# Twice x added by TensorE, the sum read from PSUM, and a tile's mean and normalisation on ScalarE

## The reference, cut to what matters

```python
xj0, xj1 = _split(node_features[col])                       # 64 scalars, 32 vectors of 3
m0, m1 = _tp(xj0, xj1, e0, e1, wm000, wm011, wm101, wm110)  # message of an edge
...
agg = segment_sum(msgs, row, num_segments=N)
u0, u1 = _tp(x0, x1, a0, a1, wu000, wu011, wu101, wu110)    # bilinear in x and agg
ud0, ud1 = _lin(x0, x1, lu0, lu1)                           # linear part
return node_features + _merge(u0 + ud0, u1 + ud1)
...
x = _layernorm(x + layer0(x, ...)); x = _layernorm(x + layer1(x, ...))
```

## Time and profile before

| what | value |
|---|---|
| median of 3 runs | 9364.85 us (9337.15 to 9369.23) |
| the profiled execution | 9380.01 us, span of its trace 9378.3 us |
| busy share of the span | PE 70%, DVE 74%, ACT 29%, POOL 47% |
| mean granted TensorE clock | 0.837 of full speed |

### The profile page before, as it was taken

How to read it: one execution, slowest core, us unless ns; L and a number is a source line. 1 busy time by engine, 2 the same in 40 slices (tenths; PEclk the granted TensorE clock), 3 DMA queues, 4 the chain that set the end, 5 groups by cost and what they waited for, 6 DMA issues and landing times.

```text
span 9378.3 us, 137567 instructions
## 1 busy us (share of the span) xinstructions
PE 6593.8 (70%) x37295; PEld 4930.3 (53%) x37295; DVE 6945.2 (74%) x8811; ACT 2700.6 (29%) x9170; POOL 4379.0 (47%) x3378
## 2 busy tenths in 40 slices
PE   3555555545554887788777887888678888888887
PEld 2443444434443655565556555656455566555665
DVE  4555555555555977777777777777489999999999
ACT  1222222222221222222222222222234444444443
POOL 1555555555555366556665666566622222222221
PEclk6777777767777988888888888888799999999999
DMA  5666565656653455555555555555321111211121
GB/s 176 197 185 187 184 185 185 197 176 187 194 185 109 141 180 177 176 184 180 177 175 184 180 178 176 183 180 180 124 77 68 66 66 66 71 66 66 66 72 46
DMA packets 692541, 1372.63 MB, mean 146 GB/s; under 512 B 106047, under 2 KB 500077, under 8 KB 666863
## 3 DMA queue, kind: packets, MB, share of 16 engines
q10 hardware_dynamic: 84636, 590.82, 20.1%
q1 hardware_dynamic: 455091, 499.42, 17.6%
q0 software_dynamic: 152736, 281.45, 9.0%
HBM read 587.20 MB, written 784.08 MB: 146 GB/s over the span
## 4 chain that ended last, share of the span: by engine, by line
PE 40%; issue 25%; DVE 18%; another core or an unknown queue 11%; ACT 3%; ACTq 1%; SPq 1%; DMA 1%; DVEq 1%; POOL 0%; POOLq 0%
PE node_ps L1169 9%; PE prods_ps L1138 7%; PE turn_ps L1158 7%; DVE work L930 6%; PE m_ps L1073 4%; DVE upd L936 3%; DVE work L917 2%; PE node_ps L1073 2%; PE node_ps L1181 2%; DVE upd L921 2%; PE s_ps L1073 2%; PE s_ps L1055 2%; PE turn_ps L1024 1%; PE prods_ps L1043 1%
## 5 line engine op out<-in xcount | busy, mean ns | idle before, releaser
L578 POOL DMA_INDIRECT slots<-pay,slot x3136 | 3259.9, 1040 | 1880.3 <-issue 1535.5
L635 POOL TENSOR_TENSOR q<-xt,yv 125x3072 f32<-125x3072 f32 x200 | 1095.6, 5478 | 3050.5 <-PE turn_ps L1158 3021.1
L1169 PE MATMUL node_ps<-msgs,onehot 128*125 128x160 f32 x6800 | 1289.6, 342 | 683.8 <-issue 665.7
L930 DVE TENSOR_TENSOR work<-prods_ps,yv 125x1024 f32<-125x1024 f32 x1200 | 1392.3, 1215 | 455.3 <-remote 439.3
L1169 PEld LDWEIGHTS node_ps<-msgs,onehot 128*125 128x125 f32 x6800 | 1154.3, 219 | 921.3 <-issue 921.1
L1139 PE MATMUL prods_ps<-w_bil,ys_t 64*125 64x512 f32 x2400 | 1372.5, 668 | 2.1 <-issue 2.1
L936 DVE TENSOR_REDUCE upd<-work 125x48 f32<-125x3072 f32 x400 | 1341.2, 3353 | 13.7
L1158 PEld LDWEIGHTS turn_ps<-ident,q 125*128 125x128 f32 x9600 | 1137.0, 196 | 181.4 <-issue 175.7
L1158 PE MATMUL turn_ps<-ident,q 125*128 125x125 f32 x9600 | 1185.9, 281 | 3.7 <-ACT q_t L1405 3.4
L1138 PE MATMUL prods_ps<-w_bil,a_t 64*125 64x512 f32 x1600 | 890.4, 660 | 325.9 <-DVE work L917 238.2
L917 DVE TENSOR_TENSOR work<-prods_ps,xt 125x1024 f32<-125x1024 f32 x800 | 956.8, 1217 | 71.2 <-issue 44.8
(11 more groups left out here) (220 smaller groups left out, 9298.1 us busy)
## 6 DMA issues: line engine op xcount, KB each, us to landing
msgs<-slots ACTq DMA_DIRECT2D x200, 1428.0 KB, 6.2
slots<-zero ACTq DMA_DIRECT2D x183, 1386.0 KB
win<-table SPq DMA_DIRECT2D x784, 160.0 KB
picks<-pick_b SPq DMA_DIRECT2D x196, 512.0 KB
pick_b<-picks SPq DMA_DIRECT2D x196, 512.0 KB
table<-tab SPq DMA_DIRECT2D x200, 350.0 KB
slots<-pay,slot POOLq DMA_INDIRECT x3136
spill_in<-spill_sums SPq DMA_DIRECT2D x200, 80.0 KB, 2.0
```

Of the source, the lines that this page charges most:

```text
L578: g.indirect_dma_start(out=slots[layer][:, :], out_offset=bass.IndirectOffsetOnAxis(ap=slot[q][:, j:j + 1], axis=0), in_=pay[q][:, j, :], ...
L635: g.tensor_tensor(q3[0:HM, :].rearrange("p (i u v) -> p i u v", i=3, u=V), xt[nb][0:HM, S:D].rearrange("p (u i) -> p i u", i=3).unsqueeze( ...
L930: ve.tensor_tensor(wk[:, i, :, :].rearrange("p w (h k) -> p h w k", h=2), prods_ps[r % 2][0:HM, :].rearrange("p (h w k) -> p h w k", h=2, ...
L1169: te.matmul(node_ps[0:HM, 0:D], onehot[:, j, :], msgs[b][:, j, 0:D], start=(j == 0), stop=False)
```

## The change

PE gets a matmul of x with twice the identity (`ident2`), 125 x 160, as the first into `node_ps` in the linear part, and the linear weights of the vector part are laid out in the order of the features (`lin_u`), so that `node_ps` then holds 2x + the linear part. In layer 1 DVE adds `node_ps` and `upd` in one instruction; in layer 0, where PE reuses the bank soon, ACT still copies it (one copy in place of two). DVE's row sum, scaling and normalisation go to ACT, which runs four activations for mean, centring, squares and root, and one more for the result. DVE keeps the reciprocal, as `inverse`, called between its multiply of round 2 and its reduce of round 1.

```diff
@@ DVE, node_step
+                if not nodes and within(t, 2, NT + 2):
+                    inverse(layer, t - 2)
...
-                        ve.wait_ge(s["h_part"], 3 * n)
+                        ve.wait_ge(s["h_ready"], n)
...
+                        if r == 2 and within(t, 2, NT + 1):
+                            inverse(layer, t - 2)
                         if r > 0:
                             ve.wait_ge(s["prods_used"], USES * n + used(r - 1))
                             ve.tensor_reduce(upd[0:HM, ROUND // S * (r - 1):ROUND // S * r], third(r - 1), AX_X, ALU.add).then_inc(s["upd"], 1)
-                if within(t, 2, NT + 2):
-                    normalise(layer, (t - 2, half - 1, b))
...
-                    ve.wait_ge(s["lin_out"], 2 * n + 2)
+                    ve.wait_ge(*((s["lin_out"], n + 1) if layer == 0 else (s["lin"], n + 1)))
                     if within(n, 1, NT):
-                        ve.wait_ge(s["normed"], 2 * n)
-                    ve.scalar_tensor_tensor(h[0:HM, :], X, 2.0, lin[0:HM, :], ALU.mult, ALU.add).then_inc(s["h_part"], 1)
+                        ve.wait_ge(s["deviation"], 4 * n - 2)
                     ve.wait_ge(s["upd"], RS_ALL * n + RS_ALL)
...
-                    ve.tensor_scalar(stats[0:HM, 1:2], stats[0:HM, 0:1], -1.0 / D, None, ALU.mult).then_inc(s["h_ready"], 1)
+                    ve.tensor_tensor(h[0:HM, :], lin[0:HM, :] if layer == 0 else node_ps[0:HM, 0:D], upd[0:HM, :], ALU.add).then_inc(s["h_ready"], 1)
...
+            def inverse(layer, n):
+                s = LS[layer]
+                ve.wait_ge(s["deviation"], 4 * n + 4)
+                ve.reciprocal(stats[0:HM, 4:5], stats[0:HM, 3:4]).then_inc(s["inverse"], 1)
@@ PE, linear
-                    te.matmul(node_ps[0:HM, S:D], v_t[:, :], w.lin1[:, :], start=True, stop=True)
-                    te.matmul(node_ps[0:HM, 0:S], ys_t[:, :], w.lin0[:, :], start=True, stop=False)
+                    te.matmul(node_ps[0:HM, 0:D], ident2[0:HM, 0:HM], xt[nb][0:HM, :], start=True, stop=False)
+                    te.matmul(node_ps[0:HM, S:D], v_t[:, :], w.lin_u[:, :], start=False, stop=False)
+                    te.matmul(node_ps[0:HM, 0:S], ys_t[:, :], w.lin0[:, :], start=False, stop=False)
@@ ACT, deviation
-                ac.activation(sq[0:HM, :], h[0:HM, :], ACT.Square, bias=stats[0:HM, 1:2], accum_out=stats[0:HM, 2:3]).then_inc(s["deviation"], 1)
-                ac.wait_ge(s["deviation"], 2 * n + 1)
+                if within(n, 1, NT):
+                    ac.wait_ge(s["normed"], n)
+                ac.activation(sq[0:HM, :], h[0:HM, :], ACT.Identity, scale=-1.0 / D, accum_out=stats[0:HM, 1:2]).then_inc(s["deviation"], 1)
+                ac.wait_ge(s["deviation"], 4 * n + 1)
+                ac.activation(centred[0:HM, :], h[0:HM, :], ACT.Identity, bias=stats[0:HM, 1:2]).then_inc(s["deviation"], 1)
+                ac.wait_ge(s["deviation"], 4 * n + 2)
+                ac.activation(sq[0:HM, :], centred[0:HM, :], ACT.Square, accum_out=stats[0:HM, 2:3]).then_inc(s["deviation"], 1)
+                ac.wait_ge(s["deviation"], 4 * n + 3)
                 ac.activation(stats[0:HM, 3:4], stats[0:HM, 2:3], ACT.Sqrt, bias=eps_col[0:HM, :], scale=1.0 / D).then_inc(s["deviation"], 1)
+            def normalise(layer, k):
...
+                ac.wait_ge(s["inverse"], n + 1)
...
+                ac.activation(res[b][0:HM, :], centred[0:HM, :], ACT.Copy, scale=stats[0:HM, 4:5]).then_inc(s["normed"], 1)
@@ ACT, node_step: linear_out
-                    if not nodes:
+                    if layer == 1 or not nodes:
                         return
...
@@ ACT, node_step: order
                 paid(0, 2)
                 paid(0, 3)
+                if within(t, 2, NT + 2):
+                    normalise(layer, (t - 2, half - 1, b))
                 features()
```

More of the change, by code:

```diff
@@ L143, in build @@
         ident = sb("ident", [P, P])
+        ident2 = sb("ident2", [P, P])
         after = sb("after", [P, P])
@@ L163, in build @@
             t.lin1 = sb(f"w_lin1{layer}", [3 * V, 3 * V])
+            t.lin_u = sb(f"w_lin_u{layer}", [3 * V, 3 * V])
             t.msg_s = sb(f"w_msg_s{layer}", [S, 2 * S + 3 * V])
@@ L246, in build @@
         sq = sb("sq", [P, D])
+        centred = sb("centred", [P, D])
         res = [sb(f"res{b}", [P, D]) for b in range(2)]
@@ L515, in node_step @@
                 if within(t, 2, NT + 2):
-                    sp.wait_ge(s["normed"], 2 * t - 2)
+                    sp.wait_ge(s["normed"], t - 1)
                     put_tile(to, (t - 2) * HM, res[b], s["stored"][b])
@@ L676, in _ @@
             ve.tensor_copy(so.rank_bound[:, :], so.rank_bound_i[:, :]).then_inc(consts, 1)
+            ve.tensor_scalar(ident2[:, :], ident[:, :], 2.0, None, ALU.mult)
             ve.wait_ge(consts, 2)
@@ L740, in scale @@
                     node = ((t.bil[:, 0:SS // 2], "u_ss"), (mix[0:S, :], "u_sv"), (mix[S:P, :], "u_vs"),
-                            (t.vv[:, :, :], "u_vv"), (t.lin0[0:S, :], "l_s"), (t.lin1[:, :], "l_v"))
+                            (t.vv[:, :, :], "u_vv"), (t.lin0[0:S, :], "l_s"))
                     for what, c in (message, node)[part]:
                         last = ve.tensor_scalar(what, what, float(k[c]), None, ALU.mult)
+                    if part == 1:
+                        last = ve.tensor_scalar(t.lin_u[:, :].rearrange("p (u i) -> p i u", i=3), t.lin1[:, :].rearrange("p (i u) -> p i u", i=3),
+                                                float(k["l_v"]), None, ALU.mult)
                 last.then_inc(w_ready, 1)
@@ L1166, in sum_edges @@
                     if within(t, 2, NT):
-                        te.wait_ge(s["lin_out"], 2 * t - 2)
+                        te.wait_ge(s["lin_out" if layer == 0 else "h_ready"], t - 1)
                     for j in range(BLOCKS):
@@ L1365, in deviation @@
                 ac.wait_ge(s["h_ready"], n + 1)
-                ac.activation(sq[0:HM, :], h[0:HM, :], ACT.Square, bias=stats[0:HM, 1:2], accum_out=stats[0:HM, 2:3]).then_inc(s["deviation"], 1)
-                ac.wait_ge(s["deviation"], 2 * n + 1)
-                ac.activation(stats[0:HM, 3:4], stats[0:HM, 2:3], ACT.Sqrt, bias=eps_col[0:HM, :], scale=1.0 / D).then_inc(s["deviation"], 1)
+                if within(n, 1, NT):
[6 more added lines that the diff above has]
+                ac.wait_ge(s["deviation"], 4 * n + 3)
+                ac.activation(stats[0:HM, 3:4], stats[0:HM, 2:3], ACT.Sqrt, bias=eps_col[0:HM, :], scale=1.0 / D).then_inc(s["deviation"], 1)
+            def normalise(layer, k):
+                n, half, b = k
+                s = LS[layer]
+                ac.wait_ge(s["inverse"], n + 1)
+                if within(n, 2, NT):
+                    ac.wait_ge(s["stored"][b], 32 * half)
+                    if layer == 0:
+                        ac.wait_ge(LS[1]["t_turned"], n - 1)
+                ac.activation(res[b][0:HM, :], centred[0:HM, :], ACT.Copy, scale=stats[0:HM, 4:5]).then_inc(s["normed"], 1)
             def node_step(layer, k, chunk):
@@ L1419, in linear_out @@
                     if within(n, 1, NT):
[L1420 to L1423, removed]
+                        ac.wait_ge(s["h_ready"], n)
+                    ac.copy(lin[0:HM, :], node_ps[0:HM, 0:D]).then_inc(s["lin_out"], 1)
                 def turned_y():
```

22 lines of the change are left out of this document (3 added, 19 removed).

## The result

The changed kernel takes 9533.17 us (median of 4 runs, 9512.82 to 9546.45) against 9365.26 beside it: 1.0188 of before, with a 95% interval of 1.0169 to 1.0207. It is 168 us slower; I had forecast 9357 and a range up to 9402. Two single executions further down, one of l1_only (10933 us) and one of l0_mean (18075 us), lie far above the others of their kernel and count in no ratio.

The account below looks back on a forecast made before the run. Layer 1 goes at DVE's pace; in layer 0 DVE waits for PE, whose resumption hangs on POOL's burst. Layer 1 -14, layer 0 +5, setup and tail +1 make -8 us: 9357 from 9365, range 9310 to 9402.

Parts of the forecast that it names:

- The step that failed: Layer 0's sweep: PE's extra matmul disappears and DVE's shorter step buys nothing; +0.05 us a step taken, +5 us in all.
- the mark of being wrong that I had named: Signs named as showing the forecast wrong: layer 0's step at 38 us, or layer 1's at 23.8 with no reciprocal idle.
- The sentence on PE: Layer 0: PE's +0.29 us behind L635's start disappears, since PE's resumption hangs on POOL's scatter burst.
- the one on DVE: Layer 0: DVE's shorter step buys nothing, as DVE waits for PE there.
- The rival "slower": Layer 0: PE's extra matmul pushes two edge matmuls behind the stall, +0.49 us a step, +48 us, 9413; chance 0.14.
- Layer 1's mechanism: Layer 1: ACT's root comes late at the reciprocal's new place, stalling DVE 1.2 us a tile; calm tiles gain nothing.
- The gain of 0.14 that I left from the meeting with POOL: Layer 1: -0.14 us a tile, -14 us over 100, from what L945's meeting with POOL cost; tile taken as 25.25.
- my other value, 25.4: Layer 1's mean tile if DVE's longer stall in late tiles also holds back round 3's multiply and PE's round 5.
- The rival "late tiles go": Layer 1: DVE's stall moves PE's idle times and late tiles may vanish, -42 to -58 us, 9310 to 9328; chance 0.20.
- The rival "the whole saving arrives": Layer 1: DVE's saving arrives whole, 1.6 us a tile, 160 us, about 9205; chance 0.05.
- my reason against it: Layer 1: the 4.3 us of room was at the reciprocal's old place; at the new one the root misses by 2.4.
- The sum's other terms: First stage untouched; setup and the last tile's longer chain add 1 us.

Follow-up runs that it names:

- l1_only: The whole change in layer 1's sweep alone, layer 0's as before, against the kernel before: ratio 0.9978, layer 1's tile 25.40 us.
- l0_mean: Layer 0 alone: mean and normalisation on ACT, reciprocal on DVE mid-rounds, twice x left on DVE; against the kernel before: ratio 0.9982.
- l0_mm0_again: The kernel before plus one matmul per tile in layer 0 (zero times identity against x), in the slower group: ratio 1.0001, step 37.54 us.
- l0_pad_again: Whole change in layer 0 alone plus one needless DVE instruction ahead of the one-hot, slower group, against the kernel before: ratio 1.0004, step 37.71 us.
- l0_only: The whole change in layer 0's sweep alone, layer 1's as before, against the kernel before: ratio 1.0138, layer 0's step 39.23 us.
- l1_late: Change in layer 1 alone, reciprocal at its old place behind the four reduces, ACT's normalisation later; against the kernel before: 0.9836, tile 23.89 us.
- l1_early: Change in layer 1 alone, with mean, deviation and root ahead of the one-hot's ReLU on ACT; against the kernel before: 0.9855, tile 24.02 us.
- l0_pad: Whole change in layer 0 alone plus one needless DVE instruction ahead of the one-hot, first try, faster group, against the kernel before: ratio 0.9957.
- l0_hotmid: The kernel before with layer 0's one-hot between round 5's last multiplies and their reduce: ratio 1.0611 in the faster group, 1.0141 in the slower.
- The best version: Twice x by TensorE in both layers, mean and normalisation on ACT in layer 1 alone, late reciprocal: 9164.74 us against 9316.14 before, 0.9840.

## Why the prediction was wrong

- **The step that failed** is layer 0's: "+0.29 on PE behind L635's start disappears in it. DVE's shorter step buys nothing either, as DVE waits for PE there", with +0.05 us a step taken. Measured were +1.63 us a step, 155 us over the layer, and the mark of being wrong that I had named, layer 0's step at 38 us, is what came. The sentence on PE holds (l0_mm0_again: 0.00); the one on DVE fails. That the resumption hangs on POOL's burst holds too: PE goes on 2.35 to 2.55 us after the last scatter in every kernel of the table. What I didn't ask is what the burst hangs on, nor how many matmuls PE gets out before it is held. DVE's shorter step moved the one-hot from 6.5 to 5.57 us, ahead of the first scatter at 5.62. Both parts of the change are needed to get there (6.2 with one, 6.0 with the other), hence no loss with either alone. That the place of the one-hot is the cause is shown by l0_pad_again. The path from there to the step is one scatter more in the unhindered run: it shows as 1.2 us at POOL and PE between l0_only and l0_pad_again. How PE's hold-up begins, and with it how many matmuls it leaves behind, was not tested by itself, and the slower clock of these matmuls was only seen beside it.
- **The rival "slower"** had the right side with the wrong mechanism: PE's extra matmul, priced at +0.49 a step, measured 0.
- **Layer 1's mechanism was right**: the root is late at its new place, 1.24 us a tile were measured for the 1.2 forecast, DVE alone would need 23.79 us and l1_late needs 23.89. The forecast of 25.25 a tile was somewhat low: l1_only has 25.40 and the whole change 25.55. The gain of 0.14 that I left from the meeting with POOL did not arrive; my other value, 25.4, was the right one. Where the 0.16 us between l1_only and the whole change comes from is open.
- **The rival "late tiles go"** was tied to the stall; they went when the stall did (l1_late, granted clock 1.00), not before.
- **The rival "the whole saving arrives"**, 9205, is about what the change gives in layer 1 with the reciprocal left in place: l1_late is 1.6% below before, 149 us. That the root is late at the new place, my reason against it, held for the change as it stands.
- The sum's other terms, 1 us for setup and tail, are too small to be seen.

## What to carry to other kernels

When a change shortens an engine's step, list what that engine does next that holds a resource shared with another, and compare its new start with the other's next start: a one-hot that starts 0.05 us ahead of the scatter, and not 0.1 behind it, cost 1.5 us a step here. A price on the engine that waits isn't enough; look also at what sets the length of the wait. And an instruction that needs a result of another engine belongs at the latest place at which its own result is still in time: the reciprocal of 0.16 us, asked for 5.2 instead of 9.7 us after the add (its places in l1_early and l1_late), ate the whole saving in l1_only.

## What the runs showed of the hardware

One kernel ran at two speeds in different groups, 9316 to 9365 us and 7703 to 7706, on the same program. The chip alone doesn't decide it: the groups at 9326 and 7706 ran on the same chip, some 18 minutes apart. In the faster one PE isn't held up in the scatters; the 34 matmuls of an edge sum run in one piece although the scatters go on (L1201; l0_pad, timeline of PE):

```profile
3410.32 4.88 PE L1201 MATMUL node_ps<-msgs,onehot 128*125 128x160 f32 x34
```

POOL's scatters take 0.96 us every 1.27 in both, DVE's one-hot 2.36 us in both, and layer 1's tile is the same. The first stage, which I did not study, differs as well: the first product of q starts 2284 to 2293 us into the program in the faster one, 2938 to 3018 in the slower. What holds PE in the slower one isn't known. It decides what a layer 0 edit is worth: l0_pad is at 0.9957 in one and 1.0004 in the other, l0_hotmid at 1.0611 and 1.0141. The best version in its form with four needless reduces gained 1.75% in the faster one, and the tile of layer 1 is 23.90 us there, so layer 1's gain holds in both. The whole change was not run in the faster one.
